# Each permutation tile of the first pass in four instructions of 512 columns in place of one of 2048

## The reference

```python
h = jnp.maximum(_layernorm(x, axis=-1), 0.0)
x = x + _L0_gnn_ref(h, edge_index, edge_weight, ...)
h = jnp.maximum(_layernorm(x, axis=-1), 0.0)
x = x + _L1_gnn_ref(h, edge_index, edge_attr_32, ...)

# L0: two GCN convolutions, relu between them, log_softmax behind them
h = x @ W
msg = h[row] * norm[:, None]
out = jax.ops.segment_sum(msg, col, num_segments=n_nodes) + b
# L1: one GIN convolution with edge attributes, an MLP and a batch norm
msg = jax.nn.relu(x[src] + edge_attr @ We + be)
aggr = jax.ops.segment_sum(msg, dst, num_segments=x.shape[0])
```

## Time and profile before

| | |
|---|---|
| median of 3 runs | 5789.29 us (5761.77 to 5809.41) |
| profiled execution: time | 5793.31 us |
| its span | 5791.5 us |
| PE, PEld busy | 4408.2 us (76%), 3394.3 us (59%) |
| DVE busy | 3686.3 us (64%) |
| ACT busy | 1291.0 us (22%) |
| POOL busy | 3759.7 us (65%) |
| mean granted clock of TensorE | 0.842 |

### The profile page before, as it was taken

One profiled execution on the slowest core, in us unless ns is written; L12 is line 12 of the kernel. 1 busy time (PEld: TensorE's weight loads), 2 busy tenths in 40 slices (PEclk: granted clock), 3 DMA queues, 4 the chain that ended last, 5 costly groups with the idle time before them and its releaser, 6 DMA issues.

```text
span 5791.5 us, 116629 instructions
## 1 busy us (share of the span) xinstructions
PE 4408.2 (76%) x29893; PEld 3394.3 (59%) x29894; DVE 3686.3 (64%) x10748; ACT 1291.0 (22%) x4287; POOL 3759.7 (65%) x3554
## 2 busy tenths in 40 slices
PE   4466666666666666679999999975888888899995
PEld 4344444444444444567777777764666666677773
DVE  3466666666666666468888888866555555566662
ACT  5111111111111111141111111125322232222223
POOL 2377777777777777656777776755544455566663
PEclk6577778777777777679999999967998898999997
DMA  2122222222222222122222222233222222222224
GB/s 53 39 48 47 47 49 47 47 50 48 46 47 46 49 48 47 42 59 51 51 51 51 52 51 50 52 85 84 58 57 55 55 57 56 56 64 64 62 61 106
DMA packets 239972, 316.92 MB, mean 55 GB/s; under 512 B 69263, under 2 KB 175178, under 8 KB 239545
## 3 DMA queue, kind: packets, MB, share of 16 engines
q0 software_dynamic: 111232, 170.85, 15.8%
q1 hardware_dynamic: 128688, 145.48, 8.7%
HBM read 276.92 MB, written 39.15 MB: 55 GB/s over the span
## 4 chain that ended last, share of the span: by engine, by line
PE 56%; POOL 14%; DVE 11%; issue 11%; DMA 3%; ACT 2%; DVEq 2%; SPq 0%; POOLq 0%; ACTq 0%
PE psum L1220 25%; PE psum L1140 14%; POOL rows_g L658 13%; PE psum L1163 6%; PE psum L1127 3%; PE psum L1084 2%; DVE x_tab L1660 2%; DMA x_more<-in_edge_attr_dram 2%; DVE rows_g L1617 1%; PE psum L1148 1%; DVEq L432 1%; PE psum L1152 1%; PE psum L1287 1%; DVE x_tab L1655 1%; DMA rows_g<-table,idx 1%
## 5 line engine op out<-in xcount | busy, mean ns | idle before, releaser
L658 POOL DMA_INDIRECT rows_g<-table,idx x3476 | 3596.6, 1035 | 1732.2 <-issue 1019.2
L1220 PE MATMUL psum<-x_tab 125*128 x8512 | 1198.6, 296 | 82.1 <-issue 43.9
L1140 PE MATMUL psum<-hot,rows_g 128*96 128x128 f32 x7512 | 1082.2, 298 | 122.8 <-DMA rows_g<-table,idx 66.6
L1140 PEld LDWEIGHTS psum<-hot,rows_g 128*96 128x96 f32 x7512 | 984.6, 181 | 216.1 <-issue 126.3
L1220 PEld LDWEIGHTS psum<-x_tab 125*128 125x128 bf16 x8512 | 851.6, 100 | 437.7 <-issue 162.1
L1163 PE MATMUL psum<-x_tab 128*104 128x512 bf16 x2432 | 618.9, 406 | 531.6 <-DVE x_tab L1660 531.6
L1580 DVE TENSOR_TENSOR acc<-acc,psum 96x128 f32 x1173 | 328.9, 280 | 965.4 <-PE psum L1140 949.2
L791 ACT ACTIVATE attr<-edge 128x12 f32 (+1 forms) x1173 | 243.5, 211 | 2951.2 <-PE psum L1140 2942.1
L1163 PEld LDWEIGHTS psum<-x_tab 128*104 128x104 bf16 x2432 | 304.9, 133 | 781.4 <-ACT x_tab L848 320.5
L1617 DVE TENSOR_REDUCE rows_g<-psum 128x384 f32<-128x1152 f32 x304 | 412.1, 1356 | 443.8 <-PE psum L1220 442.2
L1571 DVE TENSOR_SCALAR hot<-iota,attr 128x128 f32<-128x128 f32 x2504 | 685.6, 355 | 6.8 <-ACT acc L785 4.3
(11 more groups left out here) (255 smaller groups left out, 3767.3 us busy)
## 6 DMA issues: line engine op xcount, KB each, us to landing
rows_g<-table,idx POOLq DMA_INDIRECT x3476, 2.5
x_tab<-sorted_keys SPq DMA_DIRECT2D x304, 125.0 KB
x_more<-in_edge_attr_dram SPq DMA_DIRECT2D x238, 64.0 KB
sorted_attr<-x_tab SPq DMA_DIRECT2D x38, 384.0 KB, 3.0
x_more<-sorted_attr SPq DMA_DIRECT2D x152, 96.0 KB
table<-x_tab SPq DMA_DIRECT2D x13, 840.0 KB
x_tab<-in_edge_attr_dram SPq DMA_DIRECT2D x38, 256.0 KB, 2.8
x_tab<-in_x_dram SPq DMA_DIRECT2D x2, 4200.0 KB
```

The lines of the kernel that those rows point to most:

```text
L658: pool.indirect_dma_start(out=rows_g[u][0:np_, g * F:(g + 1) * F], out_offset=None, in_=table[p], in_offset=bass.IndirectOffsetOnAxis(ap=i ...
L1140: last = pe.matmul(ps_agg[t.b], rows_g[t.u][0:t.np_, g * F:(g + 1) * F], hot[t.h][0:t.np_, g, :], start=g == 0, stop=g == G - 1)
L1220: last = pe.matmul(ps_sel[c], mask[i % 2][j][:, c * P:(c + 1) * P], tab3[:, j:J - KB + 1 + j, :, :][:, bass.ds(w[c], 1), :, :].rearrange(" ...
```

## The change

The tile of a column is built by four instructions, each on 512 of its 2048 columns, one behind the other on VectorE. The scalar, the comparison and the types stay the same. The semaphore goes up once, with the last of the four, so TensorE's waits are as before.

```diff
             def sort_perm(it, c):
                 dve.wait_ge(s_permd, SC * it + c + 1)
-                dve.tensor_scalar(perm[c % 3], iota_h, rank[:, c:c + 1], None, ALU.is_equal).then_inc(s_perm, 1)
+                for b in range(4):
+                    cols = slice(b * BK, (b + 1) * BK)
+                    last = dve.tensor_scalar(perm[c % 3][:, cols], iota_h[:, cols], rank[:, c:c + 1], None, ALU.is_equal)
+                last.then_inc(s_perm, 1)
```

## The result

| | before | after |
|---|---|---|
| median (runs) | 5799.09 us (5761.77 to 5809.41, 4) | 5997.51 us (5991.89 to 6009.33, 4) |
| profiled execution, its span | 5793.31, 5791.5 us | 5996.42, 5994.6 us |
| mean granted clock | 0.842 | 0.849 |

The ratio is 1.0357, with a 95% interval of 1.0305 to 1.0408: slower by 198 us at the median and by 203 us in the two spans. The forecast was slower by 127 us: 5916 us, with 5860 to 5985 as its own range. The measured time lies above that range and inside the wider one, 5812 to 6020, whose upper end was set by the rivals.

The account below looks back on a forecast made before the run. Two near-equal first-pass loops, POOL 55.3 us and compute 54.65, bound the kernel; compute plus 3.93 makes 58.6, +3.33 x 38 = +127 us, giving 5916 us, range 5860 to 5985, 8 in 10 within 5812 to 6020.

Parts of the forecast that it names:

- Now DVE is slower than PE, so the third tile decides: First-pass three-tile steps: VectorE needs 1.04 us per tile, TensorE 0.88, so the third tile delays each step by 0.71 us.
- two near-equal loops: First-pass turn before the change: POOL's 40 gathers take 55.3 us, the loop of PE, DVE and ACT 54.65.
- undisturbed steps, 190: Steps 3 to 7 of each first-pass turn: +0.71 us in each of five, 3.55 per turn.
- rest of the turn (tile 0, slack to the gathers): Per first-pass turn: step 2's lone tile adds 0.38 us; the compute loop first has 0.60 us below POOL's loop.
- Meetings with POOL: VectorE's pieces meeting gathers: 0.02 us per piece, counted only in the upper end of 0.29 us between pieces.
- The clock: Rival, chance 0.11: TensorE falls to half clock in steps 3 to 7, 2.7 us each; one per turn gives 6019 us.
- PE's clock drops inside steps 3 to 7: Sign of being wrong: TensorE leaves full clock within the first pass's three-tile steps, which the forecast took at full clock.
- The slack: First-pass turn: the compute loop could lengthen by 0.60 us before passing POOL's loop and setting the pace.
- Short instructions seem to hold it up less, so POOL's loop should fall towards 51 us: First-pass gathers: less delay beside short pieces, POOL's loop falling from 55.3 us per turn; gain at most 0.60 us.
- The evidence from the second pass: Beside ten back-to-back L1603 a gather averages 0.975 us, against 1.077 in the first pass; taken as sign of relief.
- gathers suffer more: Rival, chance 0.10: 64 pieces per turn go before POOL, doubling its 5.3 us loss to 60.6 per turn; 5992 us.
- the compute loop becomes 54.65 + 3.93: First-pass turn of PE, DVE and ACT: lengthened by 3.93 us to 58.6, 3.33 above the turn of 55.25.

Follow-up runs that it names:

- the 44 matmuls: The changed kernel with 44 TensorE matmuls on zeros in step 2 of each first-pass turn, ahead of the wait for tile 0: 5900.29 us, ratio 1.019.
- the second measurement: The changed kernel itself, unaltered, run again beside the kernel before as yardstick for other runs: 5992.32 us, ratio 1.0367.

## Why the prediction was right, and where its sum was off

**The piece.** Forecast 0.26 us apart, the last 0.34; measured 0.263 and 0.34 undisturbed. With whole tiles at 0.663 and halves at 0.396 this is 0.13 us for each instruction and 0.26 ns a column. The Trainium skill's page "VectorE: DVE Perf Modes", section "The TRN2 errata", gives a fixed latency of 58 cycles by the table and about 150 measured; by its 0.96 GHz the trace's 0.13 us would be about 125 cycles, an estimate, nearer the second.

**The path.** "Now DVE is slower than PE, so the third tile decides": right. The undisturbed step grew by 0.74 us (forecast 0.71, or 3.55 a turn), with the gathers gone by as much; with halves, where DVE stays the faster one, by 0.13. Over 190 steps that is 141 us of the measured ones, and the forecast had 135. **The bound changed** from two near-equal loops to the compute loop alone, POOL idle for indices: right.

**Terms that were mis-sized.** A turn grew by 6.21 us (236 us in 38), not 3.33 (127 us):

| term | forecast, us | trace, us |
|---|---|---|
| undisturbed steps, 190 | 135 | 190 x 0.74 = 141 |
| pieces slower where gathers get in | 0 | 79 x (6.03 - 5.58) = 36 |
| steps partly at half clock | 0 | 43 x (7.09 - 5.58) - 14 = 51 |
| rest of the turn (tile 0, slack to the gathers) | 14 - 23 = -9 | 38 x 0.16 = 6 |
| won back at the pass's end | 0 | 205 - 236 = -31 |

7.09 is the mean of the 29 and 14 steps above, and 14 is what the 10 such steps lay above 4.84 before. The column adds up to 203, against 205 us of lag at the second pass's first gather; the 2 us between are roundings of the means.

- *Meetings with POOL.* The prediction put 0.02 us for them into its upper end, since L1660's mean exceeded its shortest by that much. In pieces it is 0.04 us wherever gathers run. In the trace, single steps from one piece to the next are 0.467 us in place of 0.263, 0.20 more where a gather gets in. And the path now goes over all twelve pieces of a step, where it went over the first tile only, so that each meeting counts. The step that failed is to have priced the meetings by how long a whole tile takes.
- *The clock* was named as a rival at "one per turn", 103 us. It came about in 43 steps, but each cost some 1.5 us in place of 2.7, because the clock fell or rose within them. So the forecast of a full-speed PE was wrong for 23% of the steps. "PE's clock drops inside steps 3 to 7" was one of the prediction's own signs of being wrong, and it showed. That the idleness before tile 0 puts the first steps at half clock is shown by the 44 matmuls, which repaired all 38; but that idleness was there before the change (8.65 us), and why 29 first steps fall now in place of 10 isn't shown, nor what lets the 14 later ones fall. The 51 us are thus counted in the trace, not isolated: 28 first steps fell in the second measurement too, but without gathers the pieces had fewer.
- *The slack.* The rest of a turn (all but the five steps) was to shrink by 0.22 us a turn, and grew by 0.16. With 44 zero matmuls it fell from 30.9 to 29.2, so half-clock work lies in it. How much of that is new with the change was not separated.
- *The pass's end* was not thought of: a pacer that is slower than the gathers lets them run ahead, and the steps without sorting cash that in. The lead is counted in the trace; no run isolates it.

**What was wrong outright** is the gathers. "Short instructions seem to hold it up less, so POOL's loop should fall towards 51 us" failed: per turn 5.3 us were lost before, 7.7 after (40 x (1.133 - 0.94)). Half of it came true: gathers of 1.0 to 1.5 us fell from 427 to 109 in 37 turns. But the piece boundaries don't let in a gather that is held; it waits for the whole run, 3.88 us where it began just ahead. The evidence from the second pass was read rightly and didn't carry over: there 270 gathers fall on runs of ten L1603, and none takes over 1.08 us. What sets L1603 apart from L1662 isn't shown; the constant in place of the scalar is one difference, the type read another. The Trainium skill, "SBUF — State Buffer", section "Who interferes with whom", speaks of a hold for one instruction; here the measurement goes further, and decides. The rival "gathers suffer more" named 5992 us, nearest of all to the 5997.51 measured, and that is luck: the gathers did lose more, with no effect on this time, because the compute loop passed them: 40 x (1.133 + 0.305) = 57.5 us lie below 61.46. But it is the floor under every repair. The kernels with a signal per piece or half removed much or all of the compute side's loss and stopped at 57.9 and 57.5, and the two with one tile in pieces at 59, with 9.3 and 9.7 us lost.

So the direction held for the reason given, and 141 of some 203 us are the mechanism that was forecast. The time lies in the wide range only because that range took in the rivals. The step "the compute loop becomes 54.65 + 3.93" carried two assumptions that it put at nothing in its middle value, undisturbed pieces and a full clock; in the trace they are 36 and 51 us.

## What to carry to other kernels

Splitting an instruction for a consumer that still waits for its last piece buys nothing and costs the fixed part of each piece; what it costs on the path is decided by whether the builder gets slower than the consumer, and then by the last tile, not the first. Where two loops are almost equally long, reckon the second one's length anew too: with VectorE's tiles in pieces the gathers' loop went from 55.3 to between 57.5 and 59.5 us, and no shorter compute loop could pass that. TensorE's waits may also be paid a second time in its clock; look at the granted clock of the steps behind the wait before you put their matmuls down at full speed.

## What the runs showed of the hardware

- A gather issue (L658) that began 0.18 us ahead of twelve L1662 back to back ended only 0.47 us behind the last of them: 3.88 us in place of 0.94. One that began 0.87 us behind the first ended 1.4 us behind the last. In other steps of the same kernel three or four get in between, not slowed (0.94 us), and VectorE then has single steps of 0.467 us in place of 0.263. On runs of ten L1603 none was held (1.08 us at most).
- A scalar read from each partition costs 0.06 us on a 512-column comparison (0.263 against 0.20 us from one to the next).
- TensorE stayed at 2.4 GHz behind 7.31 us of zero matmuls and 1.61 us of idleness, and ran at 1.2 GHz behind 3.74 us of them and 4.89 us of idleness.
- The same kernel took 7162 us on one chip and 5783 us on another. A three-tile step without gathers on the slower one took as long as a step on the other (4.83 us).
